# State-space loop of a two-layer decoder kernel: six of sixteen input products a block scaled on ScalarE with tokens as partitions and turned into PSUM by TensorE; two PSUM pairs used by turns

## The reference

```
delta = softplus(dtl @ W_dt.T + 2 * b_dt)                 # per token and channel, 512 channels
x = silu(causal_conv(repeat(x), conv_w) + conv_b)         # u below
def step(state, inp):                                     # over the 64 tokens of a sequence
    u, dlt, Bs, Cs = inp
    dA = exp(dlt[..., None] * A_g)                        # 16 states per channel
    du = dlt * u
    state = dA * state + du[..., None] * Bs[:, :, None, :]
    y = einsum('bgdn,bgn->bgd', state, Cs)
y = (y + x * D_param) * silu(z);  return y @ W_out.T
```

## Time and profile before

| | us |
|---|---|
| median of 3 runs | 991.39 (991.15 to 991.79) |
| the profiled execution | 989.19 |
| its span | 987.1 |
| busy in the span: PE, DVE, ACT, POOL | 855.6, 587.8, 428.9, 253.0 |
| the loop of 64 steps, first product to end of last scan | 36.2 to 284.3 |
| busy in 36 to 285: DVE, PE, POOL, ACT | 236.0, 199.2, 181.4, 117.6 |

### The profile page before, as it was taken

One profiled execution on the slowest core, in us unless ns is written; L12 is line 12 of the kernel. 1 busy time (PEld: TensorE's weight loads), 2 busy tenths in 40 slices (PEclk: granted clock), 3 DMA queues, 4 the chain that ended last, 5 costly groups with the idle time before them and its releaser, 6 DMA issues.

```text
span 987.1 us, 12466 instructions
## 1 busy us (share of the span) xinstructions
PE 855.6 (87%) x5135; PEld 519.6 (53%) x5138; DVE 587.8 (60%) x718; ACT 428.9 (43%) x640; POOL 253.0 (26%) x116
## 2 busy tenths in 40 slices
PE   6777887886888999999999999998998989998665
PEld 3233333332454466666666766665884656666423
DVE  3999899999991333324235445538854443345674
ACT  4754555533416555556552212224553222221476
POOL 0278687786730000000000000001049930000000
PEclk9699899998999999999999999999599999999778
DMA  9556455556734000000000420030000000000001
GB/s 314 144 131 168 128 149 140 137 150 180 206 103 171 1 1 1 1 1 2 1 1 1 186 108 1 0 128 2 3 2 1 1 1 1 1 1 1 1 6 38
DMA packets 18456, 64.40 MB, mean 65 GB/s; under 512 B 3008, under 2 KB 4672, under 8 KB 17152
## 3 DMA queue, kind: packets, MB, share of 16 engines
q1 hardware_dynamic: 18400, 63.60, 21.8%
HBM read 60.05 MB, written 3.15 MB: 64 GB/s over the span
## 4 chain that ended last, share of the span: by engine, by line
PE 60%; DVE 24%; ACT 11%; issue 4%; DMA 0%; POOL 0%; DVEq 0%; ACTq 0%
PE ps L1014 11%; PE ps L1102 11%; DVE region_c L1527 10%; DVE ps L1522 6%; PE ps L1177 6%; PE ps L1161 5%; PE ps L1061 3%; PE ps L1083 3%; PE ps L903 3%; PE ps L857 2%; ACT region_c L612 2%; PE ps L1019 2%; PE ps L988 2%; PE ps L1216 1%; PE ps L1072 1%
## 5 line engine op out<-in xcount | busy, mean ns | idle before, releaser
L1102 PE MATMUL ps<-region_c 128*128 128x256 f32 x512 | 123.3, 389 | 2.2 <-ACT region_c L612 2.2
L378 POOL TENSOR_TENSOR region_c<-region_c,region_b 128x1024 f32<-128x1024 f32 x42 | 102.8, 2447 | 80.0 <-DVE region_c L1527 59.8
L1102 PEld LDWEIGHTS ps<-region_c 128*128 128x128 f32 x512 | 100.1, 196 | 39.1 <-issue 24.0
L390 POOL TENSOR_TENSOR x<-x,region_a 128x2048 f32<-128x2048 f32 x1 | 4.5, 4533 | 384.9 <-DVE xn L1441 384.9
L1527 DVE TENSOR_TENSOR_SCAN region_c<-region_c,ps 128x1024 f32<-128x1024 f32 x43 | 98.3, 2286 | 1.5
L903 PE MATMUL ps<-region_c,ident 128*128 128x512 f32 x168 | 86.2, 638 | 6.0 <-DVE region_c L1506 6.0
L1522 DVE TENSOR_TENSOR ps<-ps,region_c 128x1024 f32<-128x1024 f32 x64 | 78.9, 1233 | 9.9 <-PE ps L891 4.9
L1604 DVE COPY region_b<-ps 128x512 f32<-128x512 f32 x32 | 21.3, 688 | 100.3 <-PE ps L1072 100.3
L891 PE MATMUL ps<-region_b,sel_b 96*128 96x512 bf16 x128 | 41.8, 410 | 42.2 <-DVE ps L1522 42.1
L1014 PE MATMUL ps<-xnT,region_c 128*128 128x512 f32 x128 | 61.4, 609 | 4.0 <-ACT region_c L612 4.0
L612 ACT ACTIVATE region_c<-ps 128x512 f32<-128x512 f32 x64 | 34.1, 598 | 67.5 <-PE ps L1083 67.5
(11 more groups left out here) (221 smaller groups left out, 1527.6 us busy)
## 6 DMA issues: line engine op xcount, KB each, us to landing
region_b<-m_rows SPq DMA_DIRECT2D x43, 512.0 KB, 4.5
region_c<-m_rows SPq DMA_DIRECT2D x21, 512.0 KB, 4.6
region_a<-in_x_wo SPq DMA_DIRECT2D x2, 2048.0 KB, 12.3
m_rows<-region_b SPq DMA_DIRECT2D x4, 512.0 KB, 5.2
region_a<-in_x_wq SPq DMA_DIRECT2D x8, 256.0 KB, 4.6
region_b<-in_f_fc SPq DMA_DIRECT2D x1, 2048.0 KB, 8.4
region_b<-in_f_proj SPq DMA_DIRECT2D x1, 2048.0 KB, 12.8
region_a<-in_x_wqT SPq DMA_DIRECT2D x1, 2048.0 KB, 15.7
```

The source lines that it names most:

```text
L378: pool.tensor_tensor(m_hc[u % 3], m_h[u % 3], m_cb[u % 3], ALU.mult).then_inc(sem("m_hc"), 1)
L1102: last = pe.matmul(tiles2(2 * (it // 4) + t // 2)[:, t % 2, :], o_T[:, a, 128 * t:128 * t + 128], wvo[:, 4 * (it % 4) + a, :], start=(it % ...
```

## The change

Of the 16 states of a block, those in `TURNED` = (3, 5, 7, 9, 11, 13) lose their DVE product. For them B * du is made with tokens as partitions, where B of a state is one number a partition: once a block PE turns `m_du` into PSUM `pair(6)` (`turn_du`, eight 128 x 128 transposes) and ACT copies it to `m_duT` (`turned_du`); for each turned step ACT scales it with eight activations of 128 x 128, one for each 128 tokens (`turned_product`, two buffers `m_dbuT` in the region of xn), and PE turns the eight tiles back into the pair that the scan reads (`put_product`). B with tokens as partitions is projected once (`turn_b`, 16 matmuls of 64 columns, and the small copy `turned_b`). The steps use PSUM `pair(0)` and `pair(2)` by turns: B, product in place and scan of step u are all in `pair(2 * (u % 2))`, so that `put_b(u)` waits for scan u - 2 and no longer for a product. The preparation of block k + 1 is moved one step later on PE, ACT, POOL and DVE.

```
+TURNED = (3, 5, 7, 9, 11, 13)
+        m_duT = view("A", 28, [NT, 128])
+        m_dbuT = [xn[:, 4 * i:4 * i + 4, :].rearrange("p t (a n) -> p (t a) n", a=2) for i in range(2)]
...
+            def turned_product(u):
+                j, i = turned_no(u), TURNED.index(u % DST)
+                act.wait_ge(sem("m_bT"), 1)
+                act.wait_ge(sem("m_duT"), u // DST + 1)
+                if j >= 2:
+                    act.wait_ge(sem("m_b"), (j - 2) // len(TURNED) * DST + TURNED[(j - 2) % len(TURNED)] + 1)
+                for t in range(NT):
+                    last = act.activation(m_dbuT[j % 2][:, t, :], m_duT[:, t, :], ACT.Copy,
+                                          scale=m_bT[:, NK * t + u // DST, i:i + 1])
+                last.then_inc(sem("m_dbuT"), 1)
...
+                if u == 0:
+                    act.wait_ge(sem("m_proj"), proj_no("BT", 0))
+                    turned_b()
+                if n == 1:
+                    turned_du(k)
+                if turned(u):
+                    turned_product(u)
                 if k < NK - 1:
-                    if n == 2:
+                    if n == 3:
                         step_in(k + 1)
...
+                elif u >= 2:
+                    pe.wait_ge(sem("m_scan"), u - 1)
+                for c in range(2):
+                    last = pe.matmul(ps[:, 2 * (u % 2) + c, :], sel_b[:, u % 32, :],
+                                     m_sb[:, u // 32, c * HALF:c * HALF + HALF], start=True, stop=True)
+                last.then_inc(sem("m_b"), 1)
+
+            def put_product(u):
+                pe.wait_ge(sem("m_dbuT"), turned_no(u) + 1)
+                pe.wait_ge(sem("m_scan"), u - 1)
+                for t in range(NT):
+                    last = pe.transpose(ps[:, 2 * (u % 2) + t // 4, 128 * (t % 4):128 * (t % 4) + 128],
+                                        m_dbuT[turned_no(u) % 2][:, t, :], ident[:, :])
+                last.then_inc(sem("m_b"), 1)
...
-                    put_b(u + 1)
+                    if turned(u + 1):
+                        put_product(u + 1)
+                    else:
+                        put_b(u + 1)
                 if u >= 2:
                     add_state(u - 2)
+                if n == 0:
+                    if k == 0:
+                        turn_b()
+                    turn_du(k)
                 if k < NK - 1:
-                    if n in (0, 1):
-                        if k == 0:
-                            pe.wait_ge(sem("m_cT"), 1)
-                        else:
-                            pe.wait_ge(sem("m_zs"), k)
-                        steps(k + 1, (n,))
-                    if n in (3, 4):
+                    if n in (1, 2):
+                        pe.wait_ge(sem("m_duT"), k + 1)
+                        steps(k + 1, (n - 1,))
+                    if n in (4, 5):
                         pe.wait_ge(sem("m_ax"), k + 2)
-                        columns("C", k + 1, (n - 3,))
...
                 dve.wait_ge(sem("m_b"), u + 1)
-                if u >= 1:
-                    dve.wait_ge(sem("m_scan"), u)
-                dve.tensor_tensor(pair(2), pair(0), m_du, ALU.mult).then_inc(sem("m_dbu"), 1)
-                dve.wait_ge(sem("m_dbu"), u + 1)
+                if not turned(u):
+                    dve.tensor_tensor(inputs(u), inputs(u), m_du, ALU.mult).then_inc(sem("m_dbu"), 1)
+                    dve.wait_ge(sem("m_dbu"), products(u))
```

More of the change, by code:

```diff
@@ L221, in pair, with turned, turned_no, products @@
             return ps[:, a:a + 2, :].rearrange("p a n -> p (a n)")
-        PROJ_ORDER = [("low rank", 0), ("B", 0), ("dt", 0), ("x", 0), ("C", 0), ("conv", 0)]
+        def turned(u):
+            return u % DST in TURNED
+        def turned_no(u):
+            return len(TURNED) * (u // DST) + TURNED.index(u % DST)
+        def products(u):
+            return sum(not turned(v) for v in range(u + 1))
+        def inputs(u):
+            return pair(2 * (u % 2))
+        PROJ_ORDER = [("low rank", 0), ("B", 0), ("dt", 0), ("x", 0), ("C", 0), ("conv", 0), ("BT", 0)]
         for k in range(NK):
+            PROJ_ORDER += [("duT", k)]
             if k < NK - 1:
@@ L236, in proj_pair @@
         def proj_pair(what, k):
-            return PROJ_PAIR[what] if k == 0 and what != "z" else 6
+            return PROJ_PAIR[what] if k == 0 and what in PROJ_PAIR else 6
         def paired(layer, it):
@@ L495, in channels, with turned_b, turned_du @@
                 act.activation(m_u[:, k, :], m_acc, ACT.Silu).then_inc(sem("m_u"), 1)
+            def turned_b():
+                act.activation(m_bT[:, :, :], ps[:, 6, :].rearrange("p (a n) -> p a n", n=DST)
+                               [:, :, TURNED[0]:TURNED[-1] + 1:2], ACT.Copy).then_inc(sem("m_bT"), 1)
+            def turned_du(k):
+                if k >= 1:
+                    act.wait_ge(sem("m_dbuT"), len(TURNED) * k)
+                act.activation(m_duT.rearrange("p t n -> p (t n)"), done("duT", k), ACT.Copy)\
+                    .then_inc(sem("m_duT"), 1)
+            def turned_product(u):
[8 more added lines that the diff above has]
+                last.then_inc(sem("m_dbuT"), 1)
             act.wait_ge(sem("m_proj"), 1)
@@ L887, in put_b, with turn_b, turn_du @@
                     pe.wait_ge(sem("ld_sb"), 96)
-                else:
[L889 to L893, removed]
+                elif u >= 2:
[11 more added lines that the diff above has]
+                last.then_inc(sem("m_b"), 1)
+            def turn_b():
+                pe.wait_ge(sem("m_cT"), 1)
+                for t in range(NT):
+                    for kh in range(KH):
+                        last = pe.matmul(ps[:, 6, 64 * t:64 * t + 64], xnT[:, kh, 128 * t:128 * t + 128],
+                                         m_win[:, kh, M_B:M_C], start=(t == 0 and kh == 0),
+                                         stop=(t == NT - 1 and kh == KH - 1), skip_group_check=True)
+                last.then_inc(sem("m_proj"), 1)
+            def turn_du(k):
+                pe.wait_ge(sem("m_du"), k + 1)
+                if k >= 1:
+                    pe.wait_ge(sem("m_zs"), k)
+                else:
+                    pe.wait_ge(sem("m_bT"), 1)
+                for t in range(NT):
+                    last = pe.transpose(ps[:, 6 + t // 4, 128 * (t % 4):128 * (t % 4) + 128],
+                                        m_du[:, 128 * t:128 * t + 128], ident[:, :])
+                last.then_inc(sem("m_proj"), 1)
             def add_state(u):
@@ L1530, in _ @@
                     skip(k - 1)
-                if n == 11 and k < NK - 1:
+                if n == 12 and k < NK - 1:
                     select_log(k + 1)
```

43 lines of the change are left out of this document (25 added, 18 removed).

## The result

| | before | after |
|---|---|---|
| median, us | 991.27 (4 runs, 991.04 to 991.79) | 1020.3 (4 runs, 1018.8 to 1020.97) |
| the profiled execution | 989.19 | 1020.97 |
| its span | 987.1 | 1018.9 |
| loop, first product to end of last scan | 36.2 to 284.3 | 38.9 to 315.3 |

The changed kernel takes 1.029 times the time of before (95% interval 1.0272 to 1.0308), 29.0 us more. In the profiled executions the loop is 276.4 long in place of 248.1, which is +28.3. The loop starts 2.7 later, and what follows it takes 703.6 in place of 702.8. Two executions further on, one of the kernel before (1736.18) and one of `m_du` at once (2717.95), ran in a slow state, and the medians given here are of the others.

What follows compares the result with a forecast made beforehand. VectorE was taken to bound the loop. New waits of 65.0 less 5.8 of before gave +59.2; less 33.0 for removed products and hand-overs, +26 on the median 991.4: 1017 us, range 994 to 1032.

Steps and rivals of the forecast that it cites:

- The likeliest case: Whole kernel at 1004 to 1024 us, chance 0.57: late ScalarE and TensorE make VectorE wait more than the removed products save.
- ScalarE's lead holds: Rival: half projection and `step_in` come through before the skip, so only 12 of new waits remain; 964 us, chance 0.10.
- Products: VectorE in the loop: 24 products go away at 1.233 each, 29.6 us less.
- Hand-overs: VectorE's gaps before and after each removed product, 0.14 a product, 3.4 us less for 24.
- In sum -33.0: All that goes away on VectorE in the loop: 29.6 of products and 3.4 of gaps round them.
- Nothing else hangs on VectorE's side: Claim that, beyond the removed products and their gaps, the removal changes nothing on VectorE; size none.
- The waits after the skip: At block heads VectorE waits for TensorE's `add_state`, delayed projection and `put_b`: 3.5 in k = 1 and 2, 2.3 in k = 3.
- The chain behind it: Later VectorE waits at a block head: 1.5 at n = 4, 4.0 at n = 5, 3.2 at n = 6, then 0.7 and 0.8.
- Prices: Cost of a turned product: eight ScalarE activations 2.44, eight TensorE transposes 1.04 at full clock, 2.0 at half.
- Outside the loop nothing changes: Claim that the rest of the kernel keeps its time, as the next stage's weight loads wait for the same last scans.
- The rival by the Trainium skill: Transposes do not count as busy for TensorE's clock: some 2 us later at five places, 5 more, 1022; no separate chance.

Runs made afterwards that it cites:

- `m_du` at once: The changed kernel without the wait of `m_du` for the last scan of the block before: 1017.28 us, and 1016.65 when run again.
- Taking the two orders back: The changed kernel, six states turned, with both halves of delta's projection ahead of the skip-dependent matmuls and both of x's ahead of `put_product(9)` in k = 1: 985.59 us.
- two-pairs kernel: The kernel before with two PSUM pairs by turns, product in place, and no VectorE wait for its own scan before a product: 981.74 us.
- the one with none turned: The kernel before with pairs by turns, delta and x projections ahead, preparation one step later, `m_du` not waiting for the scan, no turned product: 977.72 us.
- The filler kernel: The changed kernel with twelve bf16 matmuls before `put_product` waits for its input, at n = 3, 5 and n = 11 of k = 1: 1014.36 us.
- three products a block: The changed kernel with only n = 7, 11, 13 turned, delta and x projections ahead and `m_du` not waiting for the scan: 971.29 us.
- a fourth: The changed kernel with n = 7, 9, 11, 13 turned, delta and x projections ahead and `m_du` not waiting for the scan: 978.9 us.

## Why the prediction was right

+26 was forecast and +29.0 measured, at 1017 and 1020.3. The likeliest case came true by its mechanism: `step_in` waited for the half projection behind the skip, the transposes of n = 5 waited 5.38 for the activations (5.6 forecast), with the clock at half while they ran, and the longest waits of VectorE are those at n = 5 and, in k = 1, at n = 11. The waits are 61.9 (65.0 forecast), and ScalarE's busy time in the loop is 177.3 (178 forecast). Taking the two orders back gives 34.7; that was the ground on which the rival "ScalarE's lead holds" was refused.

By its steps:

- **Products.** -29.6 forecast, -30.2 measured.
- **Hand-overs, sized too small.** "In sum -33.0" has 3.4 for hand-overs, as 24 times the gap round a product. By the rows it is not a product as such that brings the gap but the wait for the scan just issued, and the two pairs took it from all 64 steps: 5.0 of idle and 2.3 of overlap here, 9.4 in all when alone. Those 3.9 more, and 0.6 of shorter products, were missed.
- **"Nothing else hangs on VectorE's side": wrong.** `m_du` and the predicated copies came to lie behind a GpSimd instruction that reads SBUF: +9.7. The diff showed the new wait ahead of `m_du`, the trace of before showed GpSimd's 3.26 beside it, and the walk should have asked what runs beside it.
- **The waits after the skip, sized too large.** 3.5 was forecast at the heads of k = 1 and 2 and 2.3 in k = 3, from a clock at half, "twice that at half". They were 1.24, 2.93 and 1.77. At k = 1 the idle of 2.40 left the clock full; at k = 2 and 3 it was at half for part of the stretch only.
- **The chain behind it.** At n = 4 it waited 1.56 (1.5 forecast), at n = 5 3.99 (4.0), at n = 6 3.4 to 3.6 (3.2), at n = 7 0.76 (0.7), at n = 9 1.02 (0.8); in k = 1 at n = 10 1.58 (1.6), at n = 11 7.45 (7.2), at n = 12 1.36 (1.4). In k = 3, 12.4 forecast, the waits are 1.77, 1.57, 1.89, 3.00, 1.58, 0.73 and 0.73, 11.3.
- **Prices.** Eight activations 2.44 (2.44), transposes 1.09 at full clock and 1.97 at half (1.04, 2.0).
- **"Outside the loop nothing changes":** the profiled executions differ there by 3.5. But the one of before, which began its loop at 36.2, was 2.2 under its own median; the two-pairs kernel and the one with none turned, with the same work ahead of the loop, began at 38.4 and 38.5, and the kernel with six turned and both projections ahead at 36.2. So that is mostly the execution, and adding the sum to the median, as was done, was right.

In sum: 26.2, less 3.9 for the pairs, less 0.6 for the shorter products, less 3.1 for the waits, plus 9.7 for the collisions gives 28.3, the growth of the profiled loop. Errors of -7.6 and +9.7 nearly cancelled; the mechanism was right, but that the time came this close is in part luck.

The rival by the Trainium skill (TensorE: Matmul & The Clock Gate, Part 4: PE-mode transpose), that the transposes would not bring the clock back: in the loop of the changed kernel it came back 3.5 to 6.0 us after the work resumed with transposes, and 2.8 and 4.0 after it resumed with `add_state`; in the kernel before, 2.9 to 5.3 after `add_state`. The two ranges overlap, so a delay of some 2 us by that rule can be neither seen nor ruled out. No run took them apart, and it stays open. The filler kernel shows only that their times at full clock are 1.09.

## What to carry to other kernels

Work is not free on an idle engine: what counts is what stands ahead of it in that engine's queue and what that waits for. ScalarE had 71 us to spare here by the prediction's sum, and the change cost 29; 35 came back when two projections went to the other side of a wait; three products a block found gaps there and a fourth did not. Price the parts of a change apart: the pairs alone gained 9.4, and six turned products a block earned nothing even with the order mended. And look at what each moved instruction then runs beside.

## What the runs showed of the hardware that I had not expected

- VectorE and GpSimd, both from SBUF: an f32 product of 128 x 1024 took 3.37 when GpSimd's had started 0.1 before it, and 1.34 when it was itself first, with GpSimd's then 3.36 in place of 2.35.
- VectorE to itself: with no wait between them a product follows the scan 2.21 after its start, though the scan's row says 2.29; with a wait for that scan's semaphore it was 2.39 (101.70 to 104.09 in the trace of before).
- TensorE's granted clock stayed at 1.00 over an idle of 2.40 and was at half after one of 5.38, and in the kernel before after one of 2.98. But there it also went to half at 162.1, after an idle of only 1.96, where the two matmuls of `put_b` took 0.98 in place of 0.60. So the length of the last idle alone does not decide it, and these rows set no limit.

```profile
161.99 0.98 PE L891 MATMUL ps<-region_b,sel_b 96*128 96x512 bf16 x2 [1.96 <-DVE ps L1522]
```
